# A graph-network kernel: sort loop in groups of four with the bias copied in by ScalarE, edge columns turned in pairs, bucket numbers loaded once a turn

## What is computed

```
def _rgcn_layer(x, src, dst, edge_type, edge_attr, W, root, bias, nn_w, nn_b):
    n = x.shape[0]
    edge_w = edge_attr @ nn_w.T + nn_b
    msg = jax.nn.relu(x[src] * edge_w)
    out = x @ root + bias
    for r in range(N_REL):
        mask = edge_type == r
        m = jnp.where(mask[:, None], msg, 0.0)
        s = jax.ops.segment_sum(m, dst, num_segments=n)
        cnt = jax.ops.segment_sum(mask.astype(x.dtype), dst, num_segments=n)
        mean = s / jnp.maximum(cnt, 1.0)[:, None]
        out = out + mean @ W[r]
    return out
...
gate = jax.nn.sigmoid(jax.nn.silu(rbf @ W1 + b1) @ W2 + b2)
msg = gate * h[src]
aggr = jax.ops.segment_sum(msg, dst, num_segments=h.shape[0])
```

## Time and profile before

| | us |
|---|---|
| median of 3 runs | 4751.31 |
| lowest, highest | 4744.28, 4754.04 |
| span of the profiled execution | 4744.9 |
| sort loop | about 172 to 780 |
| layers 0, 1, 2 | 787 to 1345, 1455 to 1950, 2058 to 2555 |
| gated layer, gathering part | 2665 to 3175 |

### The profile page before, as it was taken

One profiled execution on the slowest core, in us unless ns is written; L12 is line 12 of the kernel. 1 busy time (PEld: TensorE's weight loads), 2 busy tenths in 40 slices (PEclk: granted clock), 3 DMA queues, 4 the chain that ended last, 5 costly groups with the idle time before them and its releaser, 6 DMA issues. The chain is left out here.

```text
span 4744.9 us, 105920 instructions
## 1 busy us (share of the span) xinstructions
PE 3915.0 (83%) x22300; PEld 3233.3 (68%) x22301; DVE 3382.7 (71%) x9318; ACT 1791.0 (38%) x5399; POOL 3071.7 (65%) x3178
## 2 busy tenths in 40 slices
PE   6799997889987889878899566779978778578886
PEld 3477775778776778767777556668866666366664
DVE  7799997667757778677787667874257778756666
ACT  0355553221123333333333100004257667367774
POOL 0266665777756777567775777766777773067774
PEclk9799998999998999989999777888978898778787
DMA  1233334856626445264452687861465444144445
GB/s 47 92 131 131 130 132 130 212 126 158 152 63 202 135 145 154 71 185 146 145 149 78 208 257 214 245 191 54 145 182 120 105 106 125 32 99 109 109 109 100
DMA packets 643665, 643.00 MB, mean 136 GB/s; under 512 B 314342, under 2 KB 549540, under 8 KB 643396
## 3 DMA queue, kind: packets, MB, share of 16 engines
q0 software_dynamic: 145840, 374.54, 27.8%
q1 hardware_dynamic: 443348, 213.36, 17.0%
q10 hardware_dynamic: 54336, 53.65, 3.3%
HBM read 470.09 MB, written 170.26 MB: 135 GB/s over the span
## 5 line engine op out<-in xcount | busy, mean ns | idle before, releaser
L1059 POOL DMA_INDIRECT G<-h_dram,idx x1572 | 1525.8, 971 | 556.8 <-issue 361.6
L1283 PEld LDWEIGHTS ps_a<-hotm,msg 128*128 128x128 f32 x4716 | 686.5, 193 | 196.2 <-DVE arena L1395 67.5
L1283 PE MATMUL ps_a<-hotm,msg 128*128 128x128 f32 x4716 | 730.0, 282 | 88.5 <-DVE arena L1395 87.8
L1271 PE MATMUL ps_e<-nnw,attT 128*128 128x256 f32 x2358 | 738.4, 396 | 76.8 <-DVE prodm L1388 42.4
L1395 DVE TENSOR_TENSOR arena<-ps_a,arena 128x256 f32 x1404 | 586.9, 418 | 218.8 <-issue 94.1
L735 POOL DMA_INDIRECT rec_dram<-rec,pos x392 | 376.7, 961 | 398.6 <-ACT rec L606 307.7
L1059 POOL DMA_INDIRECT G<-feat_dram,idx x420 | 402.4, 958 | 325.5 <-POOLq L241 197.9
L1317 ACT ACTIVATE msg<-prodm 128x256 f32<-128x256 f32 x786 | 327.5, 417 | 677.8 <-DVE prodm L1388 586.1
L749 POOL DMA_INDIRECT rec_dram<-rows,place x392 | 379.8, 969 | 222.1 <-issue 117.4
L1897 POOL DMA_INDIRECT arena<-rel_dram,idx x393 | 385.0, 980 | 128.6 <-issue 86.2
L1271 PEld LDWEIGHTS ps_e<-nnw,attT 128*128 128x128 f32 x2358 | 370.3, 195 | 118.4 <-DVE prodm L1388 56.4
(11 more groups left out here) (365 smaller groups left out, 7691.6 us busy)
## 6 DMA issues: line engine op xcount, KB each, us to landing
gate<-rec_dram SPq DMA_DIRECT2D x126, 384.0 KB
G<-msg_dram SPq DMA_DIRECT2D x300, 128.0 KB, 2.2
msg_dram<-msg ACTq DMA_DIRECT2D x270, 128.0 KB
rel_dram<-stage SPq DMA_DIRECT2D x25, 1040.0 KB
G<-h_dram,idx POOLq DMA_INDIRECT x1572
aT<-edge_attr SPq DMA_DIRECT2D x98, 128.0 KB
msg_dram<-arena ACTq DMA_DIRECT2D x90, 128.0 KB
attT<-attT_dram SPq DMA_DIRECT2D x74, 144.0 KB
```

The lines of the kernel that those rows point to most:

```text
L1059: pool.indirect_dma_start(G[:, n % width, :], None, table, bass.IndirectOffsetOnAxis(ap=idx[:, which, n:n + 1], axis=0)).then_inc(sem(f"sw ...
L1271: t.matmul(ps_e[s % BANKS][:], attT[:, s // HU, s % HU, :], nnw[:], start=True, stop=True).then_inc(sem("ew"), 1)
L1283: last = t.matmul(ps_a[s % BANKS][:, h, :], of[:, h * P:(h + 1) * P], hot[:, s, :], start=True, stop=True)
```

## The change

**Sort loop.** A step is now a whole group. `ps_z` takes a group at once, so `sig` and `silu` are two operations of 512 columns instead of four of 256. The bias no longer enters by a matmul: ScalarE copies `b2` (now loaded to all partitions) into `ps_g` after each gate sigmoid has read it. VectorE makes the one-hots of group g + 1 in step g, in one operation from `keys4` instead of two, and collects the source positions for one addition at the end. SP waits for `z` of group g - 2 and for `a32` of group g - 2, as before; ScalarE's copy to `rec` stands in the step after, behind the first gate sigmoid of its group and the bias copy.

```diff
-    for c0, c1, c2 in walk(nc.scalar, NG // 2, 0, 1, 2, width=PAIRS):
...
-                nc.scalar.activation(rec[:, s // 2, at:at + 2, 0:D], ps_g[s % 2][:], ACT.Sigmoid).then_inc(sem("gate"), 1)
-            if c0 and c0[2] % 2 == 1:
...
-                nc.scalar.copy(rec[:, b, :, WA32:WA32 + A32], at32[:, b, :, :]).then_inc(sem("a32"), 1)
+    for c0, c1 in walk(nc.scalar, NG // 2, 0, 1, width=2):
+        if c0:
+            g, i, b = c0
+            act.wait_ge(sem("z"), upto(g))
+            act.wait_ge(sem("silu"), upto(g - 2))
+            for h in range(DH):
+                last = nc.scalar.activation(by_pairs(sig, b, h), first_layer(b, h), ACT.Sigmoid, bias=b1[:, h:h + 1])
+            last.then_inc(sem("sig"), 1)
+        if c1:
+            g, i, b = c1
+            for q in range(2):
...
+                act.wait_ge(sem("g"), g * 2 + q + 1 + CREDIT)
+                nc.scalar.activation(rec[:, b, 2 * q:2 * q + 2, 0:D], ps_g[q][:], ACT.Sigmoid).then_inc(sem("gate"), 1)
+                act.wait_ge(sem("gate"), g * 2 + q + 1 + CREDIT)
+                nc.scalar.copy(ps_g[q][:], bias2).then_inc(sem("seeded"), 1)
+                if q == 0:
+                    nc.scalar.copy(rec[:, b, :, WA32:WA32 + A32], at32[:, b, :, :]).then_inc(sem("a32"), 1)
```

TensorE's step in the new code (the old one had, for each pair, `z`, the bias, `g` and a half of the counting). The lines left out of it are the matmuls into `ps_r` and `ps_z`, which are those of before:

```diff
+    if c0:
+        g, i, b = c0
+        pe.wait_ge(sem("hot"), g + 1)
...
+        pe.wait_ge(sem(f"attr_in{b}"), i * 32 + 32)
+        pe.wait_ge(sem("silu"), upto(g - 2))
...
+        last.then_inc(sem("z"), 1)
+    if c1:
+        g, i, b = c1
+        pe.wait_ge(sem("silu"), upto(g))
+        for q in range(2):
+            pe.wait_ge(sem("seeded"), g * 2 + q + 1)
+            for j in range(2):
+                for h in range(DH):
+                    last = t.matmul(ps_g[q][:, j, :], silu[:, b, h, 2 * j + q, :], W2[:, h, :], start=False,
+                                    stop=(h == DH - 1), skip_group_check=True)
+            last.then_inc(sem("g"), 1)
+    if c0:
+        g, i, b = c0
+        pe.wait_ge(sem("looked_up"), g + 1)
```

```diff
-    t.transpose(ps_t[:, s % 2, :], att[:, s, :], ident[:]).then_inc(sem("attT"), 1)
+    t.transpose(ps_t[:], att[:, s - s % 2:s - s % 2 + 2, :].rearrange("p s w -> p (s w)"),
+                ident[:]).then_inc(sem("attT"), pair_size(c0))
...
-    t.matmul(ps_e[s % BANKS][:], attT[:, s // HU, s % HU, :], nnw[:], start=True, stop=True).then_inc(sem("ew"), 1)
+    rows = slice(s % 2 * HALF, s % 2 * HALF + A32 + 1)
+    t.matmul(ps_e[s % BANKS][:], attT[rows, s // 2, :], nnw[rows, :], start=True, stop=True).then_inc(sem("ew"), 1)
...
-    v.memset(arena[:, 0:half], 0.0).then_inc(sem("zeroed"), 1)
+    v.memset(att[:, :, A32:A32 + 1], 1.0)
+    v.memset(att[:, :, A32 + 1:HALF], 0.0).then_inc(sem("atts_set"), 1)
     dve.wait_ge(sem("meta_in"), 16)
     v.tensor_copy(idx[:, 0, 0:U], meta[:, 0:U, 1]).then_inc(sem("columns"), 1)
-    v.memset(arena[:, half:KD * D], 0.0).then_inc(sem("zeroed"), 1)
...
+    v.memset(arena[:], 0.0).then_inc(sem("zeroed"), 1)
```

**Bucket numbers.** In layers 0 to 2 and the gated layer:

```diff
-    bucket = Buckets(nc, mybir.EngineType.DVE, bmap[0:1, 0, :], KD - 1, 8, part=HU)
+    bucket = Buckets(nc, mybir.EngineType.DVE, bmap[0:1, 0, :], KD - 1, 8, part=U)
```

More of the change, by code:

```diff
@@ L284, in credit, with sort_edges @@
                 eng.sem_inc(sem(name), CREDIT)
-        def sort_edges(nnw, attT):
+        def sort_edges(nnw):
             ctx = ExitStack()
@@ new lines, in _ @@
+                                dve.wait_ge(sem("hot"), g + 1)
+                                dve.wait_ge(sem("before"), g + 1)
+                                left = ps_r[:, :, 0:KD]
+                                v.tensor_tensor(moved[:], left, thr[:, 0:1, :].to_broadcast([P, SG, KD]), ALU.is_ge).then_inc(sem("moved"), 1)
+                                v.tensor_tensor(prod[:, b, :, KD:K], ps_r[:, :, KD:K], OK[:, b, :, KD:K], ALU.mult)
+                                dve.wait_ge(sem("moved"), g * 3 + 1)
@@ new lines, in _ @@
+                                dve.wait_ge(sem("sig"), upto(g))
+                                dve.wait_ge(sem("g"), (g - 1) * 2 + CREDIT)
+                                for h in range(DH):
+                                    last = v.scalar_tensor_tensor(by_pairs(silu, b, h), first_layer(b, h), b1[:, h:h + 1],
+                                                                  by_pairs(sig, b, h), ALU.add, ALU.mult)
+                                last.then_inc(sem("silu"), 1)
+                                dve.wait_ge(sem("counted"), g + 2)
@@ L1070, in first_turn, with ends_pair, pair_size @@
             return isinstance(unit[1], int) and unit[1] == 0
+        def ends_pair(c):
+            return c and not c.extra and (c[2] % 2 == 1 or c.late and c[2] == FRONT - 1)
+        def pair_size(c):
+            return c[2] % 2 + 1
         def gathered_by(passes, s):
@@ L1304, in _ @@
[L1304 to L1311 removed]
+                                        act.wait_ge(sem("attT"), upto(c0.m))
@@ new lines, in _ @@
+                                        seam = c0.late and isinstance(i, int) and i == SEAM and s % 2 == 0
+                                        act.wait_ge(sem("ew"), upto(turn_before(c0) + (1 if seam else 0)))
+                                        for h, (lo, hi) in enumerate(PIECES1):
+                                            if s - s % 2 == lo and not (isinstance(i, int) and i == 0):
+                                                act.wait_ge(sem(f"att_out{h}"), i * 16)
+                                        nc.scalar.copy(attT[:, s // 2, :], ps_t[:]).then_inc(sem("attT_sb"), pair_size(c0))
@@ L2433, in build @@
             nnw = sb(ctx, "nnw", [P, D])
-            attT = sb(ctx, "attT", [P, 2, HU, P])
-            sort_edges(nnw, attT)
+            attT = sb(ctx, "attT", [P, HU, P])
+            sort_edges(nnw)
             rgcn(nnw, attT)
```

291 lines of the change are left out of this document (113 added, 178 removed).

## The result

The changed kernel takes 5794.45 us (median of 4 runs, 5773.35 to 5906.79) against 4750.11 us: a ratio of 1.218, with a 95% interval of 1.214 to 1.222. It is slower, as forecast, but by 1044 us (1025 from that median) where 111 were forecast, and far outside the range. The profiled execution has a span of 5773.2 us, 1028.3 longer than that of before.

The account below looks back on a forecast made before the run. TensorE was taken to bound the sort loop, POOL the layers' early turns, TensorE and VectorE the late ones. Terms summed to +111 on a span of 4744.9, 4856; with 6.4 for the median, 4862 us; range 4800 to 4990.

Parts of the forecast that it names:

- Matmuls of 33 rows have the same columns: 0.: Edge matmul in the layers: cutting its rows to 33 leaves the columns the same, so costs 0 us.
- the chain: Sort loop: z, W2, gate, bias copy, a32 copy, SP's loads, next z follow one another and set the period.
- the forecast of 7.13: Sort loop: period in us per group, summed link by link, against 5.62 of TensorE's work and 6.08 before.
- the second rival: Sort loop: TensorE's clock falls in the new gaps, +70 to +130 us in half the groups, 4930 to 4990; chance 0.18.
- 103: Sort loop: us added over 98 groups as the period grows from 6.08 to 7.13; bounds +70 and +150.
- -6.6: Ahead of the sort loop: without its block, the loop starts 6.6 us earlier.
- 0 to +1: Ahead of the sort loop: cost in us of the nnw loads beside the x transfer.
- the earlier first gathers: Layer 0: first gather can start some 6 us earlier, without waiting behind a memset; gain 4.3 us.
- the transposes' -7: Layer 0: 393 transposes become 197, counting only in late turns; 25 us at most, taken as -7.
- the third rival: Bucket loads: register loads cost by the load, saving 34 us where +20 was forecast, so 4808; chance 0.10.
- The sum was +22: Bucket loads of 18: +20 us for three layers (bounds -30 and +35), +2 for early turns and the gated layer.
- The first rival: Sort loop: the loads arrive in time and TensorE stays the bound, giving 4714 us, faster; chance 0.09.

Follow-up runs that it names:

- experiment 9: Loads of b2 and nnw moved behind x, in the changed kernel with 128 rows, split SP loads, nine bucket numbers and early pair turning: 4691.84 us.
- bU: The kernel before with its bucket numbers loaded once a turn, 18 at a time, and nothing else: 4802.19 us, ratio 1.0106.
- asplit: The changed kernel, still with 33 rows, with SP's two loads of a group given separate waits and semaphores: 5563.66 us.
- experiment 2: The changed kernel with the edge matmul over all 128 rows of a pair, nnw standing twice with zeros elsewhere: 4973.56 us, ratio 1.047.

## Why the prediction was wrong

**The step that failed** is one half-sentence: "Matmuls of 33 rows have the same columns: 0." The columns are the same, and so is the shortest duration of a row, 376 ns after and 379 before, but two other things are not. The first is the spacing of starts at full clock: 1.26 us a chunk instead of 0.89, because the weights wait 0.3 us where 33 rows and 128 rows follow each other. The second is the clock that the chip then grants: 0.66 instead of 0.97 in layer 1. The edit was costed by its columns, and the clock was taken as given by gaps alone; it was asked for the sort loop and the gated layer, and not for the one stage in which the matmuls changed their shape. The runs put 732 us on the edit in the kernel before and 802 in the changed one. At full clock a chunk of 1.26 us still fits into POOL's 1.27 us a gather; at the low clock it is 2.30, so that TensorE sets the early turns too. That the clock stays low because TensorE then does less in a microsecond is a reading of these rows, and no run isolates it.

**The sort loop: right in its mechanism, too small.** Every link of the chain is there. Sorted by the clock granted in each, the 97 spacings between the issues of L588 are 70 at full clock with a mean of 7.35 us, 25 with a stretch at the low clock with 8.82, and the first two, 17.3 us together. At full clock the largest miss in the forecast of 7.13 is from the second issue to z: 1.65 + 0.1 forecast, 1.98 in the median (410.06 - 408.12 = 1.94 above). The earlier trace rows showed when the queues went quiet, and not when z could start. In the group above the two z take 1.09 us where 1.28 were forecast, and W2 to the gate 2.03 where 1.92 were; such misses nearly cancel, which was luck. The whole is 97 x 0.22 = 21 us. The 25 slower groups are the second rival, the clock that falls in the new gaps: with the first two they make 39 us. It had a chance of 0.18 and came about in part, in a quarter of the groups and not in half. Together 103 + 21 + 39 = 163, where 166 were measured, since the period of before is 6.04 and not 6.08. The Trainium skill's rule (TensorE: Matmul & The Clock Gate, What's actually happening) by which this rival would give nothing does not hold here: each of the 25 falls came behind gaps of 1.7 to 2.1 us, though most groups with the same gaps have none.

**Ahead of the loop**: -6.6 was forecast for the block that goes, and nothing came: the first block ends at 31.2 us instead of 26.3, which is 4.9 of it, and the other 1.5 are not traced. SP's queue issues the x load (first row after, second before) behind b2, now to 128 partitions:

```profile
11.68 6.71 SPq L374 DMA_DIRECT2D X<-x  x1
```

```profile
12.07 4.88 SPq L377 DMA_DIRECT2D X<-x  x1
```

It takes 1.8 us longer, and with `b2` and `nnw` behind it most of the 5 us came back (experiment 9). "0 to +1" for the new loads should have been +5, most of it for `b2`, which the forecast did not price.

**Layer 0**: the earlier first gathers are there. The last load of the sort loop and the first gather are 33.1 us apart instead of 39.8. Of the transposes' -7 nothing shows. In their place stand the later step and the later turn, +32 us with all else mended. The diff said both; the forecast only counted instructions and not who is then late.

**Bucket loads**: the third rival falls. Those of layer 1 after, min/median/max:

```profile
L189 DVEq TENSOR_LOAD <-bmap x25: 1417/1746/4453, 1832.6 to 2593.7; - x25
```

They go by the number and by its place, as read from the earlier trace rows. The Trainium skill's 200 ns a register (Runtime: NRT & Kernel Launch, Instruction fetch mechanics) is near the slow ones, 4.45 / 18 = 247 ns at most in this row, and not the fast ones, some 90. The sum was +22, 20 of it for three layers, and the kernel lost 50: the gathers of layers 0, 1 and 2 in bU take 12, 17 and 16 us more than before, where some 6 each were forecast. The gaps were sized right (3.13 and 0.63 us); missing was what the clock does behind a gap of 3 us.

**The first rival** (the loads arrive in time) did not come about. Its condition was right, though: in asplit they do arrive in time, and the period is 5.49 where 5.62 was given.

**The range**, 4800 to 4990, was built from the terms that had been found. Several of these missed too: the sort loop with 166 lies above its +150, the bucket loads with 50 above their +35, and layer 0 cost time where it was to save 11. With the 128 rows back (experiment 2) they make 4974 us, inside the range and 112 above the forecast. The one term that had been set to zero in half a sentence carried four fifths of the result.

## What to carry to other kernels

When an edit changes the shape of a matmul, ask for the spacing of starts beside its neighbours and for the granted clock of that stage, and not only for columns or durations: cutting the contraction rows that were only zeros looks free and made a stage here half as long again (496 to 763 us). Padding the operands with zero rows was the cheaper form. Where buffers are two, a load that waits for a late reader should not share its semaphore or its wait with one that the bound engine needs; splitting them turned +166 us into -53.

## What was not expected of the hardware

- Among matmuls of 128 rows, one of 33 or 64 rows costs more at full clock than one of 96 or 128: the next weights start 304 ns after it instead of 2, and a chunk in layer 1 is 1.26 us instead of 0.89. The durations of the rows do not show it.
- TensorE's granted clock went down with the rows that one matmul uses, with the same columns and the same number of instructions: 0.69, 0.79, 0.94, 0.97 for 33, 64, 96, 128 rows in layer 1, and 5486, 5130 to 5211, 4764 and 4752 us for the kernel. Rows of zeros count as rows.
- A register load's price is by the number, and falls from some 230 to 90 ns each by where the first one stands; a load of 18 mostly takes 4.05 to 4.45 us or some 1.6 (up to 5.3 early in a layer of bU).
- The clock fell behind gaps of 1.7 to 2.1 us in a quarter of the sort loop's groups, and behind each of the seven gaps of 2.9 to 3.1 us in the late turns of layer 1 of bU.
